# One matmul of 490 columns per pair, three banks in turn, for a graph network's relation adjacency

## The chip, the cores and the metric

The kernel runs on one core of a Trainium2 chip. The metric is the device time of one launch in microseconds (us). The kernel before was timed in three runs: 7019.02, 7025.52 and 7033.47 us, median 7025.52.

Engine names are those of the profile: PE is TensorE (PEld its weight loads), DVE VectorE, ACT ScalarE, POOL GpSimd, SP SyncE. The granted TensorE clock is given as a share of full speed; it has two levels, 0.5 (1.2 GHz) and 1.0 (2.4 GHz), and a mean over a stretch lies between them.

## The reference, cut to what matters

6250 nodes with 128 features, 206,250 edges. Each edge has one of five types (relations), each node one of three types.

```
x = layernorm(x + SAGE(SAGE(x)))            # two SAGE layers, mean over incoming edges
h = concat(x, node_emb[node_type])          # 256 features
h = relu(rgcn(h, W1, root1))                # 256 -> 256
h = relu(rgcn(h, W2, root2))                # 256 -> 128
h = rgcn(h, W3, root3)                      # 128 -> 128
out = layernorm(x + relu(h))

def rgcn(x, W, root):                       # per destination node n, per relation r
    agg[n, r] = mean of x[src] over edges into n with type r
    return sum_r agg[n, r] @ W[r] + x @ root + bias
```

## The kernel before, in words

The kernel sorts and codes the edges, runs the two SAGE layers (up to about 1480 us in the profile), and then the three relational layers, which the code calls conv 0, 1 and 2. Conv 0 ends near 4150 us.

**Groups.** In conv 0, edges are taken 512 at a time (a *group*, 403 in all). POOL fetches the source rows of a group with four indirect DMAs (L1395) into `messages`, a ring of six groups: POOL may fetch group i only when PE has finished group i-6 (`group_psum`). DVE makes a one-hot matrix of the group's destinations (L1669). PE multiplies the two, 12 matmuls of 120 columns (L1408) and four narrow ones for the node types (L1412), which raise `group_psum`. DVE adds the result to running sums (`add`, L1690 and L1691); PE needs `sums_added` of two groups back.

**Windows.** The sums of 256 nodes (a *window*, about 16 groups) are finished in 12 steps, n = 0 to 11, one per *half tick*; there are two half ticks to a group. At step 0 DVE scales the sums (`scale`, L1730, then two memsets and `node_hot`), and SP copies the scaled type sums to other partitions with six small DMAs (L1305). At step 1 PE computes the 256 wide features in two halves (L1495, L1496; between the halves it waits for SP's copies, `typed_in`, before L1493). ACT evicts them into `h_wide` (L1601). At step 3 PE computes the next layer's root part (L1502, bank 5) and then the first tile of the next layer's table (`table`, L1473, banks 6 and 7). At step 4 ACT evicts both (L1605, L1582), at step 5 DVE takes the remainder (L1747), at step 6 PE computes the second tile.

**The relations' adjacency.** Beside this, 336 of the 403 groups each carry two *couples*, and a couple is two *pairs* of nodes. For each pair DVE makes two one-hot matrices (L1678, L1679) and PE multiplies them (`build`, L1428); the result, 128 x 490 counts, is cast to 8 bits and stored for convs 1 and 2. The 490 columns are five relations of 98. Before the change they are cut in two parts, 250 and 240 columns, for the two halves of the node tiles: a couple is four matmuls, two of 250 columns (both pairs) into bank 2 and two of 240 into bank 3. ACT evicts bank 2 (L1558) and DVE bank 3 (L1560) into `stage`; every eight couples ACT stores a stage to memory (L1572). Each bank is used by every couple, so a couple's first matmul waits for ACT's eviction of the couple before, and its third for DVE's.

**Order.** All engines run the same loop over half ticks, written out at build time, and each engine keeps its order. PE in an even half tick: group, build, window step; in an odd one: build, window step. DVE: eviction of the couple of the half tick before, then (even) one-hots and `add` or (odd) the pairs' one-hots, then the window step. ACT: eviction of this half tick's couple, then the window step. Step 0 falls on an odd half tick, so step 1 follows a group and a build on PE, and on DVE the eviction that this build waited for stands behind step 0.

Of the kernel before, what the change touches and what calls it, by code (L numbers as in the profile page):

```python
# [176 lines left out]
def resnorm_gnn(nc, a, out):  # L177
# [27 lines left out]
    with ctx:  # L205
# [1011 lines left out]
        REL_BANKS, PART_BANKS = DENSE_BANKS, TABLE_BANKS  # L1217
# [180 lines left out]
        def conv_tensor(pe):  # L1398
# [17 lines left out]
            def build(j):  # L1416

                b, m = divmod(2 * j, BATCH)
                if m == 0:
                    pe.wait_ge(rel_hot_made, b + 1)  # L1420
                for n in range(SLICES):
                    if j:
                        pe.wait_ge(rel_evicted[n], j)
                    of_part = slice(2 * SLICE_FIRST[n], 2 * (SLICE_FIRST[n] + SLICE_TILES[n]))
                    width = 2 * SLICE_TILES[n] * RELATIONS
                    for q in range(2):
                        hot = rel_hot[:, b % 2, m + q, :].rearrange("p (r c) -> p r c", r=RELATIONS)[:, :, of_part]
                        mm = pe.matmul(bank[REL_BANKS[n]][:, q * width:(q + 1) * width], lo_dense_hot[:, b % 2, m + q, :], hot, start=True, stop=True)  # L1428
                    mm.then_inc(rel_psum, 1)

            def dense(v, step):
# [8 lines left out]
                if at == 0:  # L1440
                    if K >= 2:
                        pe.wait_ge(dense_kept, K - 1)
                    else:
                        pe.wait_ge(rel_evicted[K], COUPLES)
# [21 lines left out]
            def table(w, t):  # L1466
                n = w * WINDOW_TILES + t
                pe.wait_ge(wide_made, w + 1)
                pe.wait_ge(rest_made, ROW_SPLITS + n)
                nodes = slice(t * P, (t + 1) * P)  # L1470
                for b, cols in enumerate((slice(0, FIRST_CUT), slice(FIRST_CUT, RELATIONS * FEAT))):
                    for half in range(2):
                        mm = pe.matmul(bank[TABLE_BANKS[b]][:, 0:cols.stop - cols.start], h_wide[:, half, nodes], w2[:, half, cols], start=(half == 0), stop=(half == 1))  # L1473
                mm.then_inc(table_psum, 1)

            def finish(v, i, n):
# [4 lines left out]
                if v == 0:  # L1481
# [16 lines left out]
                    if n == 3:  # L1498
                        pe.wait_ge(wide_made, w + 1)
                        pe.wait_ge(root_kept, w)  # L1500
                        for half in range(2):
                            mm = pe.matmul(bank[ROOT_BANK][:, 0:cols], w2_root[:, half, :], h_wide[:, half, 0:cols], start=(half == 0), stop=(half == 1))  # L1502
                        mm.then_inc(root_psum, 1)
                        table(w, 0)
# [43 lines left out]
        def evict(engine, n, j):  # L1548

            u, m = divmod(j, STAGE_COUPLES)  # L1550
            engine.wait_ge(rel_psum, j * SLICES + n + 1)
            if m == 0 and u >= 2:
                engine.wait_ge(stage_out[u % 2], 16 * SLICES * (u // 2))
            rows = slice(RELATIONS * SLICE_FIRST[n], RELATIONS * (SLICE_FIRST[n] + SLICE_TILES[n]))
            from_bank = bank[REL_BANKS[n]][:, 0:4 * SLICE_TILES[n] * RELATIONS].rearrange("p (q c d) -> p c q d", q=2, d=2)
            to = stage[:, u % 2, rows, 4 * m:4 * m + 4].rearrange("p c (q d) -> p c q d", q=2)
# [5 lines left out]
        def conv_scalar(act):  # L1562
            def store_stage(u):
# [3 lines left out]
                for n in range(SLICES):  # L1567
                    width = SLICE_TILES[n] * STAGE_NODES
                    first = SLICE_FIRST[n] * CHUNK + s * width
                    rows = slice(RELATIONS * SLICE_FIRST[n], RELATIONS * (SLICE_FIRST[n] + SLICE_TILES[n]))  # L1570
                    of_part = stage[:, u % 2, rows, :].rearrange("p (r h) d -> p r (h d)", r=RELATIONS).bitcast(bf16)
                    act.dma_start(relations_d[c, :, :, first // 2:(first + width) // 2], of_part).then_inc(stage_out[u % 2], 16)  # L1572

            def row_pieces(w, t, step):
                n = w * WINDOW_TILES + t
                rows = table_rows[:, n % 2, :].rearrange("p (r k f) -> p r k f", r=RELATIONS, f=P)
                if step == 0:
# [3 lines left out]
                    for b, at_r, count in ((0, 0, 3), (1, 3, 2)):  # L1581
                        op = act.copy(rows[:, at_r:at_r + count, 0, :], bank[TABLE_BANKS[b]][:, 0:count * P].rearrange("p (r f) -> p r f", f=P))  # L1582
# [5 lines left out]
            def finish(v, i, n):  # L1588
# [4 lines left out]
                if v == 0:  # L1593
# [9 lines left out]
                    if n == 4:  # L1603
                        act.wait_ge(root_psum, w + 1)
                        act.activation(root_part[:, nodes], bank[ROOT_BANK][:, 0:cols], ACT.Identity, bias=bias[:, 4:5]).then_inc(root_kept, 1)  # L1605
# [55 lines left out]
        def conv_vector(vec):  # L1661
# [78 lines left out]
            def row_pieces(w, t, at_step):  # L1740
                n = w * WINDOW_TILES + t
                rows = table_rows[:, n % 2, :].rearrange("p (r k f) -> p r k f", r=RELATIONS, f=P)
                if at_step == 0:
                    vec.wait_ge(high_made, ROW_SPLITS + n + 1)
                    vec.wait_ge(low_made, ROW_SPLITS + n)
                    for b, at_r, count in ((0, 0, 3), (1, 3, 2)):
                        op = vec.tensor_tensor(rest_w[:, at_r * P:(at_r + count) * P].rearrange("p (r f) -> p r f", f=P),  # L1747
                                               bank[TABLE_BANKS[b]][:, 0:count * P].rearrange("p (r f) -> p r f", f=P), rows[:, at_r:at_r + count, 0, :], ALU.subtract)
# [436 lines left out]
```

## Time and profile before

| | |
|---|---|
| median of three runs | 7025.52 us (7019.02 to 7033.47) |
| span of the profiled execution | 7027.7 us |
| PE busy | 4925.6 us (70%) |
| POOL busy | 3636.8 us (52%) |
| DVE busy | 2875.6 us (41%) |
| ACT busy | 1023.1 us (15%) |
| mean granted TensorE clock | 0.842 |

The span is 2.2 us above the median and within the range of the runs; the page shows nothing of that execution outside its span. Shares of the whole span mix stages: the change acts on conv 0 alone, and there a view cut to 1480 to 3720 us (groups with builds) and one to 3720 to 4150 us (the last groups, without builds, and the end of the last windows) tell more.

### The profile page before, as it was taken

Reading aid. Unit: us, or ns where it says so; the run is one execution under the profiler, and the core shown is the slowest. Engines: PE = TensorE matmul, PEld = TensorE weight load, DVE = VectorE, ACT = ScalarE, POOL = GpSimd, SP = SyncE. Lnnn points to the kernel's source line nnn. Section 1 sums busy time; section 2 is a strip of 40 time slices with the busy share of each in tenths; the row PEclk is TensorE's granted clock in tenths of the full one; section 3 lists DMA queues with packets and bytes.
Section 4 is the critical chain, followed back from the end, with each engine's and each line's share of the span. In section 5 each row is a group of like instructions: output and inputs, shape, how many; then the busy total and the mean of one; then the engine's idle time right before and its main releaser. Section 6 shows DMA issues by size and latency. Waiting matters only on the chain.

```text
span 7027.7 us, 95103 instructions
## 1 busy us (share of the span) xinstructions
PE 4925.6 (70%) x35932; PEld 3076.0 (44%) x35932; DVE 2875.6 (41%) x8139; ACT 1023.1 (15%) x2385; POOL 3636.8 (52%) x3575
## 2 busy tenths in 40 slices
PE   2776789955655655656554448888888788888887
PEld 1544556633333333333333334444444445544544
DVE  5766661136666666666662211111112212111212
ACT  2544440002222222212220000000000000000000
POOL 4000000036666666666666646666666566666664
PEclk6888889977777777777776669999999899999999
DMA  2222216543434434434343334554545444444443
GB/s 77 96 111 100 90 64 227 219 135 113 121 106 120 120 105 122 119 112 117 114 116 97 97 116 134 168 167 148 169 137 167 154 138 146 138 139 147 142 135 104
DMA packets 428468, 904.12 MB, mean 129 GB/s; under 512 B 71170, under 2 KB 335116, under 8 KB 406124
## 3 DMA queue, kind: packets, MB, share of 16 engines
q0 software_dynamic: 169216, 348.44, 18.4%
q1 hardware_dynamic: 129028, 454.04, 17.7%
q10 hardware_dynamic: 129768, 95.53, 4.3%
q8 instruction: 289, 4.73, 0.3%
q14 instruction: 167, 1.37, 0.1%
HBM read 692.22 MB, written 205.05 MB: 128 GB/s over the span
## 4 chain that ended last, share of the span: by engine, by line
PE 43%; another core or an unknown queue 15%; issue 9%; DVE 8%; ACT 2%; DVEq 1%; DMA 0%; SPq 0%; ACTq 0%; POOL 0%; POOLq 0%
PE bank L1450 23%; PE bank L1408 7%; PE bank L1428 5%; PE bank L1495 2%; PE bank L1473 2%; PE bank L1412 2%; ACT stage L1558 1%; DVE stage L1560 1%; DVE scaled L1730 1%; DVE rel_hot L1679 1%; DVE type_scaled L1730 1%; DVE lo_dense_hot L1678 1%; DVE sums L1691 1%; DVE sums L1737 1%
## 5 line engine op out<-in xcount | busy, mean ns | idle before, releaser
L1395 POOL DMA_INDIRECT messages<-table,src_rows x2552 | 2653.3, 1040 | 1384.9 <-issue 692.0
L1450 PE MATMUL bank<-slices,pieces 128*128 128x384 fp8e4 x10290 | 1978.4, 337 | 375.5 <-issue 361.2
L1450 PEld LDWEIGHTS bank<-slices,pieces 128*128 128x128 bf16 x10290 | 988.8, 100 | 1211.6 <-issue 704.5
L1428 PE MATMUL bank<-rel_hot,lo_dense_hot 128*128 128x240 bf16 (+1 forms) x2688 | 589.2, 331 | 914.5 <-ACT stage L1558 463.2
L1395 POOL DMA_INDIRECT messages<-table,rel_rows x940 | 899.5, 957 | 560.8 <-issue 250.7
L1691 DVE TENSOR_TENSOR sums<-sums,bank 128x120 f32 x873 | 236.4, 271 | 2292.1 <-remote 1826.1
L1408 PE MATMUL bank<-group_hot,messages 128*128 128x120 bf16 x10476 | 832.5, 239 | 238.8 <-issue 112.8
L1408 PEld LDWEIGHTS bank<-group_hot,messages 128*128 128x128 bf16 x10476 | 747.4, 111 | 357.1 <-issue 204.8
L1428 PEld LDWEIGHTS bank<-rel_hot,lo_dense_hot 128*128 128x128 bf16 x2688 | 193.0, 106 | 1243.6 <-ACT stage L1558 532.2
L1377 POOL IOTA iota_rel_i<- 128x490 int32 x1 | 1.4, 1394 | 1355.2 <-DMA table<-typed_rows 1355.2
L1558 ACT CAST stage<-bank 128x500 fp8e4<-128x500 f32 x672 | 387.2, 576 | 1772.5 <-PE bank L1428 1094.9
L1560 DVE CAST stage<-bank 128x480 fp8e4<-128x480 f32 x672 | 435.0, 647 | 242.7 <-PE bank L1428 219.4
L877 PE MATMUL bank<-adjacency,x_pieces 128*128 128x384 bf16 (+1 forms) x2499 | 485.2, 336 | 0.0
L1679 DVE TENSOR_SCALAR rel_hot<-iota_rel,rel_dense 128x490 bf16<-128x490 f16 x1344 | 468.5, 349 | 0.0
L975 ACT CAST adjacency<-bank 128x400 bf16<-128x400 f32 x784 | 392.0, 504 | 440.4 <-PE bank L853 434.4
L1690 DVE TENSOR_TENSOR type_sums<-type_sums,bank 3x120 f32 x403 | 107.1, 266 | 812.0 <-remote 591.9
L853 PE MATMUL bank<-q_hot,lo_hot 128*128 128x100 bf16 x3136 | 230.9, 222 | 267.5 <-DVE rd_hot L1057 258.8
L877 PE MATMUL bank<-adjacency,h_pieces 128*128 128x384 bf16 (+1 forms) x2499 | 398.9, 320 | 0.0
L1678 DVE TENSOR_SCALAR lo_dense_hot<-iota,lo_dense 128x128 bf16<-128x128 f16 x1344 | 354.9, 264 | 0.0
L1669 DVE TENSOR_TENSOR group_hot<-iota,group_code 128x480 bf16<-128x480 f16 x873 | 349.5, 401 | 1.6
L853 PEld LDWEIGHTS bank<-q_hot,lo_hot 128*128 128x128 bf16 x3136 | 193.1, 105 | 344.3 <-DVE rd_hot L1057 258.7
L877 PEld LDWEIGHTS bank<-adjacency,h_pieces 128*128 128x128 bf16 x2499 | 238.5, 98 | 151.8 <-issue 3.8
(251 smaller groups left out, 3593.3 us busy)
## 6 DMA issues: line engine op xcount, KB each, us to landing
slices<-relations_d SPq DMA_DIRECT2D x70, 1200.0 KB
slices<-relations_d SPq DMA_DIRECT2D x70, 1152.0 KB
adjacency_d<-adjacency SPq DMA_DIRECT2D x15, 4704.0 KB, 14.5
adjacency<-adjacency_d SPq DMA_DIRECT2D x15, 4704.0 KB, 15.0
relations_d<-stage ACTq DMA_DIRECT2D x84, 500.0 KB
messages<-table,src_rows POOLq DMA_INDIRECT x2552
relations_d<-stage ACTq DMA_DIRECT2D x84, 480.0 KB
inverse<-inverse_d SPq DMA_DIRECT2D x52, 640.0 KB
```

The source lines that it names most:

```text
L853: mm = pe.matmul(to[:, m * PAIR_COLS:(m + 1) * PAIR_COLS], lo_hot[:, i % 2, pair, :], q_hot[:, i % 2, pair, :], start=True, stop=True)
L877: mm = pe.matmul(bank[SUM_BANKS[k % 2]][:, 0:cols], pieces[:, h, piece, :], adjacency[HALF[c]][:, h, 0:cols], start=(m == 0), stop=(m == N ...
L975: act.copy(to, pairs).then_inc(evicted, 1)
L1395: pool.indirect_dma_start(messages[:, i % MESSAGES, t, 0:ROWS[v]], None, GATHERED[v], bass.IndirectOffsetOnAxis(ap=rows[:, e:e + 1], axis= ...
L1408: mm = pe.matmul(to[:, 0:GROUP_COLS], messages[:, i % MESSAGES, t, piece * P:(piece + 1) * P], group_hot[:, i % MESSAGES, t, :], start=(t ...
L1428: mm = pe.matmul(bank[REL_BANKS[n]][:, q * width:(q + 1) * width], lo_dense_hot[:, b % 2, m + q, :], hot, start=True, stop=True)
L1450: mm = pe.matmul(bank[DENSE_BANKS[K % 2]][:, 0:CHUNK], pieces[M % PIECE_RING][:, tile % PIECE_TILES, piece * P:(piece + 1) * P], slice_of_ ...
L1558: engine.copy(to, from_bank, saturate=False).then_inc(rel_evicted[n], 1)
L1560: engine.tensor_copy(to, from_bank, saturate=False).then_inc(rel_evicted[n], 1)
L1669: vec.tensor_tensor(group_hot[:, i % MESSAGES, :, :].rearrange("p k (c t) -> p k c t", t=2), iota16[:, 0:GROUP_COLS].rearrange("p (c t) -> ...
L1678: vec.tensor_scalar(lo_dense_hot[:, b % 2, m, :], iota16[:, :], lo_dense[:, b * BATCH + m:b * BATCH + m + 1], None, ALU.is_equal)
L1679: op = vec.tensor_scalar(rel_hot[:, b % 2, m, :], iota_rel[:, :], rel_dense[:, b * BATCH + m:b * BATCH + m + 1], None, ALU.is_equal)
```

## The change

Each pair becomes one matmul of 490 columns into a bank of its own. Three banks (2, 3, 5) are taken in turn; ACT evicts the even pair of each couple and DVE the odd one. Since the banks rotate by three and the evictions by two, an even pair's matmul waits for DVE's eviction of the odd pair two couples back, an odd pair's for ACT's eviction of the couple before. `stage` holds the 245 rows in one block; an eviction writes two bytes per row where it wrote four, and the store to memory reads the two parts out of the block.

Bank 5 had been the root part's. The root part now sits in columns 0 to 255 of bank 6, and the table's second part in columns 256 to 511 of it. So the table waits for ACT's eviction of the root part (`root_kept`), the root part waits until DVE has read the tables of the window before, and the table's first tile moves from step 3 to step 4.

```diff
-        REL_BANKS, PART_BANKS = DENSE_BANKS, TABLE_BANKS
+        PART_BANKS = TABLE_BANKS
+        REL_BANKS = (2, 3, 5)
+        ROOT_1 = bank[6][:, 0:WINDOW]
+        TABLES_1 = (bank[7][:, 0:3 * P], bank[6][:, WINDOW:WINDOW + 2 * P])
...
-                for n in range(SLICES):
-                    if j:
-                        pe.wait_ge(rel_evicted[n], j)
-                    of_part = slice(2 * SLICE_FIRST[n], 2 * (SLICE_FIRST[n] + SLICE_TILES[n]))
-                    width = 2 * SLICE_TILES[n] * RELATIONS
-                    for q in range(2):
-                        hot = rel_hot[:, b % 2, m + q, :].rearrange("p (r c) -> p r c", r=RELATIONS)[:, :, of_part]
-                        mm = pe.matmul(bank[REL_BANKS[n]][:, q * width:(q + 1) * width], lo_dense_hot[:, b % 2, m + q, :], hot, start=True, stop=True)
-                    mm.then_inc(rel_psum, 1)
+                for q in range(2):
+                    pair = 2 * j + q
+                    before = pair - len(REL_BANKS)
+                    if before >= 0:
+                        pe.wait_ge(rel_evicted[before % 2], before // 2 + 1)
+                    pe.matmul(bank[REL_BANKS[pair % len(REL_BANKS)]][:, 0:REL_COLS], lo_dense_hot[:, b % 2, m + q, :], rel_hot[:, b % 2, m + q, :],
+                              start=True, stop=True).then_inc(rel_psum, 1)
...
                 pe.wait_ge(rest_made, ROW_SPLITS + n)
+                pe.wait_ge(root_kept, w + 1)
...
                         pe.wait_ge(wide_made, w + 1)
-                        pe.wait_ge(root_kept, w)
+                        pe.wait_ge(rest_made, ROW_SPLITS + w * WINDOW_TILES)
                         for half in range(2):
-                            mm = pe.matmul(bank[ROOT_BANK][:, 0:cols], w2_root[:, half, :], h_wide[:, half, 0:cols], start=(half == 0), stop=(half == 1))
+                            mm = pe.matmul(ROOT_1[:, 0:cols], w2_root[:, half, :], h_wide[:, half, 0:cols], start=(half == 0), stop=(half == 1))
                         mm.then_inc(root_psum, 1)
+                    if n == 4:
                         table(w, 0)
...
-            engine.wait_ge(rel_psum, j * SLICES + n + 1)
+            pair = 2 * j + n
+            engine.wait_ge(rel_psum, pair + 1)
...
-            rows = slice(RELATIONS * SLICE_FIRST[n], RELATIONS * (SLICE_FIRST[n] + SLICE_TILES[n]))
-            from_bank = bank[REL_BANKS[n]][:, 0:4 * SLICE_TILES[n] * RELATIONS].rearrange("p (q c d) -> p c q d", q=2, d=2)
-            to = stage[:, u % 2, rows, 4 * m:4 * m + 4].rearrange("p c (q d) -> p c q d", q=2)
+            from_bank = bank[REL_BANKS[pair % len(REL_BANKS)]][:, 0:REL_COLS].rearrange("p (c d) -> p c d", d=2)
+            to = stage[:, u % 2, :, 4 * m + 2 * n:4 * m + 2 * n + 2]
...
```

What PE has in its order around the first window's step 1, before the change (`scaled_144` is the window's scaled sums, `bank4` the wide features, `rel_evicted0` ACT's evictions and `rel_evicted1` DVE's):

```order
L1412 MATMUL bank1<-group_hot_147,messages_146 3x120 x4
L1428 MATMUL bank2<-rel_hot_154,lo_dense_hot_153 128x250 [waits rel_evicted0,rel_hot_made]
L1428 MATMUL bank2<-rel_hot_154,lo_dense_hot_153 128x250
L1428 MATMUL bank3<-rel_hot_154,lo_dense_hot_153 128x240 [waits rel_evicted1]
L1428 MATMUL bank3<-rel_hot_154,lo_dense_hot_153 128x240
L1495 MATMUL bank4<-scaled_144,w1_126 128x256 [waits wide_made,emb_in,scaled_made]
```

And after it:

```order
L1415 MATMUL bank1<-group_hot_147,messages_146 3x120 x4
L1429 MATMUL bank2<-rel_hot_154,lo_dense_hot_153 128x490 [waits rel_evicted1,rel_hot_made]
L1429 MATMUL bank3<-rel_hot_154,lo_dense_hot_153 128x490 [waits rel_evicted0]
L1498 MATMUL bank4<-scaled_144,w1_126 128x256 [waits wide_made,emb_in,scaled_made]
L1498 MATMUL bank4<-scaled_144,w1_126 128x256 x4
```

Four matmuls of the build became two, and the wait for `rel_evicted1` in front of the wide features is now for an eviction one couple older.

PE around steps 3 and 4 of the same window before the change (`w2_root_129` marks the root part, `w2_128` the table):

```order
L1428 MATMUL bank3<-rel_hot_154,lo_dense_hot_153 128x240
L1502 MATMUL bank5<-h_wide_142,w2_root_129 128x256 [waits root_kept,wide_made]
L1502 MATMUL bank5<-h_wide_142,w2_root_129 128x256
L1473 MATMUL bank6<-w2_128,h_wide_142 128x384 [waits rest_made,wide_made]
L1473 MATMUL bank6<-w2_128,h_wide_142 128x384
L1473 MATMUL bank7<-w2_128,h_wide_142 128x256 x2
L1428 MATMUL bank2<-rel_hot_154,lo_dense_hot_153 128x250 [waits rel_evicted0]
```

And after it:

```order
L1505 MATMUL bank6<-h_wide_142,w2_root_129 128x256 [waits rest_made,wide_made]
L1505 MATMUL bank6<-h_wide_142,w2_root_129 128x256
L1429 MATMUL bank2<-rel_hot_154,lo_dense_hot_153 128x490 [waits rel_evicted1]
L1429 MATMUL bank3<-rel_hot_154,lo_dense_hot_153 128x490 [waits rel_evicted0]
L1476 MATMUL bank7<-w2_128,h_wide_142 128x384 [waits root_kept,rest_made,wide_made]
L1476 MATMUL bank7<-w2_128,h_wide_142 128x384
L1476 MATMUL bank6<-w2_128,h_wide_142 128x256 x2
L1411 MATMUL bank1<-group_hot_147,messages_146 128x120 [waits gathered5,group_hot_made,sums_added]
```

The table's first tile moved behind the next couple's build, and it now waits for `root_kept`, an eviction that ACT makes in the same half tick.

## Rows read from the trace of the kernel before

**Rows 1.** Stretches: us, then busy us (instructions) per engine, granted clock, DMA share, GB/s.
```profile
1480.00:3720.00 2240.00, 1300.16 (x9074) 819.94 (x9075) 1454.38 (x4642) 459.36 (x855) 1505.97 (x1379) 0.74 0.40 116
3720.00:4150.00 430.00, 179.47 (x1258) 132.62 (x1258) 105.08 (x261) 20.36 (x44) 239.93 (x241) 0.64 0.31 87
```

**Rows 2.** Waits of POOL, 1480 to 3720 us: us in total, times, longest.
```profile
POOL messages L1395 <- issue: 376.6, 1233, 0.5
POOL messages L1395 <- PE bank L1412: 203.3, 64, 9.2
POOL messages L1395 <- remote: 147.6, 81, 4.4
```

**Rows 3.** Waits of PE in the same stretch.
```profile
PE bank L1428 <- ACT stage L1558: 463.2, 187, 19.1
PE bank L1428 <- DVE stage L1560: 233.0, 163, 8.7
```

**Rows 4.** POOL's groups (busy us, mean ns | idle), 1480:3720, then 3720:4020.
```profile
L1395 POOL DMA_INDIRECT messages<-table,src_rows x1378 | 1505.1, 1092 | 727.5 <-issue 376.6 <-PE bank L1412 203.3 <-remote 147.6
...
L1395 POOL DMA_INDIRECT messages<-table,src_rows x197 | 198.2, 1006 | 103.1 <-issue 55.8 <-remote 25.2 <-PE bank L1412 22.1
```

**Rows 5.** Stretches between two stops of POOL that end with "remote".
```profile
2224.90:2242.80 17.90, 9.31 (x72) 5.56 (x72) 10.90 (x40) 3.49 (x7) 12.61 (x12) 0.69 0.36 108
...
3741.40:3770.30 28.90, 8.44 (x80) 6.49 (x80) 3.87 (x15) 0.00 (x0) 19.14 (x20) 0.56 0.27 69
4809.50:4821.40 11.90, 9.58 (x71) 5.39 (x69) 2.33 (x7) 0.00 (x0) 7.57 (x8) 1.00 0.55 186
```

**Rows 6.** Timeline of a window with builds: start, us, instruction, idle before and releaser.
```profile
2285.81 2.36 DVE L1730 TENSOR_TENSOR scaled<-sums,inverse 128x1280 f32<-128x1280 f32 x1
...
2288.05 2.40 DVE L1730 TENSOR_TENSOR type_scaled<-type_sums,inverse 3x1280 f32<-3x1280 f32 x1
...
2294.24 0.58 PE L1428 MATMUL bank<-rel_hot,lo_dense_hot 128*128 128x240 bf16 x2 [8.65 <-DVE stage L1560]
...
2294.62 4.48 PE L1495 MATMUL bank<-scaled,w 128*128 128x256 f32 x10
...
2299.72 0.29 PEld L1493 LDWEIGHTS bank<-type_scaled,emb 18*128 18x128 f32 x2 [0.49 <-DMA type_scaled<-node_hot]
...
2300.34 2.42 PE L1495 MATMUL bank<-scaled,w 128*128 128x256 f32 x10
...
2305.56 0.94 POOL L1395 DMA_INDIRECT messages<-table,src_rows  x1 [6.49 <-PE bank L1412]
...
2308.68 0.59 PE L1428 MATMUL bank<-rel_hot,lo_dense_hot 128*128 128x250 bf16 x4
...
2311.59 0.94 POOL L1395 DMA_INDIRECT messages<-table,src_rows  x1 [1.21 <-PE bank L1412]
```

**Rows 7.** Timeline of a window without builds.
```profile
3783.84 4.32 PE L1495 MATMUL bank<-scaled,w 128*128 128x256 f32 x10 [8.45 <-DVE type_scaled L1730]
...
3792.63 1.22 PE L1493 MATMUL bank<-type_scaled,emb 18*128 18x256 f32 x2 [4.04 <-DMA type_scaled<-node_hot]
...
3793.78 4.47 PE L1495 MATMUL bank<-scaled,w 128*128 128x256 f32 x10
...
3801.21 0.94 POOL L1395 DMA_INDIRECT messages<-table,src_rows  x1 [2.84 <-PE bank L1412]
```

**Rows 8.** Stretches from L1493 to the end of the wide features.
```profile
2299.70:2303.75 4.05, 4.05 (x17) 2.78 (x16) 0.00 (x0) 0.00 (x0) 0.00 (x0) 1.00 0.12 29
3792.60:3799.20 6.60, 6.57 (x16) 4.45 (x16) 0.00 (x0) 0.00 (x0) 4.54 (x5) 0.59 0.33 83
```

**Rows 9.** Line L1605, the root part's eviction, 1480 to 3720 us: ns min/median/max.
```profile
L1605 ACT ACTIVATE root_part<-bank,bias x20: 479/479/479, 1660.8 to 3709.4; 128x256 f32<-128x256 f32 x20
```

**Rows 10.** The page's groups: busy us, mean ns, then idle us before.
```profile
L1558 ACT CAST stage<-bank 128x500 fp8e4<-128x500 f32 x672 | 387.2, 576 | 1772.5 <-PE bank L1428 1094.9
L1560 DVE CAST stage<-bank 128x480 fp8e4<-128x480 f32 x672 | 435.0, 647 | 242.7 <-PE bank L1428 219.4
```

## What the change should do to the time: the prediction

> **What bounds the kernel now.** I cut the trace by stage first. The change acts on conv 0, and nearly all of it on the 2240 us in which groups carry builds [rows 1]. PE is busy for 1300 us of them, DVE for 1454, ACT for 459: none is full. POOL is busy for 1506 us, has another 377 us in short pauses between two issues, and waits for 351 us: 203 us for PE's L1412, the last matmul of a group, and 148 us for "remote" [rows 2]. The first two make 1883 us, the third 351 us; together that is the stage. The gathers are in order and POOL waits for nothing else, so POOL paces conv 0. The time moves by what the change does to those 351 us and to POOL's own work, and by nothing else.
>
> Then I read PE's waits. PE waits 463 us for ACT's evictions and 233 us for DVE's [rows 3]. This is what the change takes away, and it looks like a tenth of the run. The reader is to see that these 696 us are not POOL's 351 us. POOL waits for a finished group when its ring of six is full, and most of PE's waits fall where PE is ahead of POOL anyway.
>
> The third view is the pace where nothing else disturbs it. POOL stops for "remote" about every third group. From stop to stop PE does 72 matmuls in 17.9 us with builds (12 fetches, three groups), 80 in 28.9 us without builds (20 fetches, five groups), 71 in 11.9 us in conv 1 (eight fetches, two groups) [rows 5]. That is 5.97, 5.78 and 5.95 us per group. Two things follow. The stops seem to come with a count of PE's instructions; what they are, these rows don't tell. And the pace per group hardly depends on what PE has to do: taking all builds away from PE, DVE and ACT gains 0.19 us per group.
>
> The fourth view is one window's timeline. POOL's long stop, 6.49 us, falls here: DVE scales from 2285.81 on, PE stands 8.65 us at a build for the DVE eviction behind that, then does the wide features, and only the next group releases POOL [rows 6]. There are 20 such windows in the stage [rows 9]. Twenty times 6.49 is 130 of the 203 us.
>
> **The change part by part.**
>
> *Builds.* Of four matmuls per couple two go, but no columns: 980 before and after. A couple takes 0.59 us at full clock [rows 6]. A matmul of 490 columns is not in the trace; I bound a couple between 0.4 us (980 columns at 2.4 GHz) and 0.6. It saves at most 0.2 us x 672 = 134 us of PE work, all of it beside POOL's fetches. In the sum: 0. If the cover were gone, 0.2 us per build behind a POOL stop, a few us.
>
> *Evictions.* ACT goes from 500 to 490 elements (576 ns), DVE from 480 to 490 (647 ns) [rows 10]. By elements that is -0.01 and +0.01 us. Two-byte writes at a step of 32 bytes are not in the trace; DVE's scaling reads with a step at 2360 ns for 1280 elements [rows 6], 1.84 ns each against 1.35 here, so at worst a DVE eviction costs 0.9 us, 0.25 more. DVE is busy for 1454 of 2240 us; two evictions per group, 0.5 us of 5.97, disappear in its idle time. In the sum: 0, at worst about 0.25 us x 20 in front of the windows.
>
> *Waits of PE on evictions.* Gone nearly everywhere. What is late next between windows is POOL itself. The gain is bounded by the no-build pace: 0.19 us x about 240 groups that lie between the windows (336 less 20 x 5) = 46 us; nothing excludes a zero. A group now has 20 matmuls in place of 24, a third of the way to the 16 without builds, and no eviction waits, so I take half of 46: -23 us.
>
> *The wide features.* Here the wait of 8.65 us goes and another takes its place. PE can start the first half as soon as DVE has scaled, at 2288.05 + 2.40 = 2290.45 in place of 2294.62. But the second half needs SP's copies, and those hang on DVE alone: L1493's weights already waited 0.49 us for the DMA in this window [rows 6]. So the second half starts at most 0.5 us earlier, and PE stands for some 4 us in front of it. The windows without builds show that very situation: first half right behind the scaling, then 4.04 us of idling for the DMA, then the same ten matmuls of L1495 in 4.47 us where they took 2.42 [rows 6, 7]. The granted clock is 0.59 in that stretch, 1.00 in the window with builds, and the way from L1493 to the end of the wide features takes 6.60 us against 4.05 [rows 8]. That is 2.55 us more less up to 0.5: 2.1 us per window, in front of the group that releases POOL. 20 x 2.1 = +42 us. Bounds: 0 if the clock holds, 20 x 2.55 = +51.
>
> The Trainium skill speaks against this part too: "TensorE: Matmul & The Clock Gate", section "HAM oscillation — how this bites in real kernels", says that a wait for a DMA between two bursts of matmuls sends the array back to half clock, burst after burst. By that rule every one of the 20 windows pays, 20 x 2.1; the trace agrees with it in the stretch at 0.59 [rows 8].
>
> *Root part and table.* The table's first tile now stands behind a build and behind ACT's eviction of the root part. PE before: root, table, build (0.59 us), next group [rows 6]. After: root, build, wait, table, group. The wait: ACT first evicts the even pair of that same build (0.3 us until its matmul is done, 0.58 us of work), then the root part (0.48 us) [rows 9, 10], and a few tenths for semaphores: 1.45 us from the root's end, of which the build covers 0.5 to 0.6. So the table starts 0.85 us later than PE could. Behind it waits the second group of the window, and POOL stood 1.21 us for that group [rows 6], where a plain pause is 0.3. So it is on the path: 20 x 0.85 = +17 us. Bounds 0 and 20 x 1.45 = +29. DVE's L1747 and the second tile move by the same, not once more. In the last windows, without builds, only ACT's 0.48 us count, and at the very end alone they are on the path: +1. The new wait of the root part on the tables of the window before is long met.
>
> *Stores, bank reuse later.* The store has the same bytes and the same number of pieces. Convs 1 and 2 use banks 2, 3, 5, 6 as before, after all evictions. 0.
>
> Sum: -23 + 42 + 17 + 1 = +37 us. The profiled span is 7027.7, 2 us above the median; applied to the median 7025.5 it gives 7062. Its own range, with the bounds: from 7025 - 46 + 0 + 0 = 6980 to 7025 + 0 + 51 + 29 = 7105; more narrowly 7040 to 7085.
>
> **The rivals.**
>
> *Faster: PE gets to the window with POOL less far ahead.* Without builds POOL's stop at the window is 2.84 us, not 6.49, although the clock is down there too [rows 6, 7]. The reason is that PE had come closer to POOL by then, so the ring had more room. If the shorter build does the same by half, each window gains (6.49 - 2.84) / 2 = 1.8 us plus the 2.1 us that I charged, and pays 0.85: against my sum -3.9 x 20 = -78, so 7062 - 78 = 6984. For it: 20 matmuls per group in place of 24 fit the count of 72 with 3.6 groups, so stops may come every fourth group. Against it: between stops DVE has 10.90 / 3 = 3.6 us of work per group that stays [rows 5], and a fetch by POOL takes 1092 ns with builds against 1006 without [rows 4]. Over four fetches that is 0.34 us per group, more than the 0.19 by which the pace differs. On this the Trainium skill has a rule, "SBUF — State Buffer", section "Who interferes with whom": DVE in its two-port modes locks GpSimd out for a whole instruction, while PE and ACT wait for nobody. By it the gain without builds is DVE's, whose work the change leaves, and this rival would be worth nothing; the means of rows 4 agree with it but do not prove it.
>
> *No change.* The clock drops, but POOL's stop is as long as before because the lag of PE shrinks by as much, and the root wait hides in POOL's "remote" stop right behind it: -23 + 42 - 20 = about 0, 7025.
>
> *More slower than I say.* If PE's idling lowers the clock in every group too (mean 0.74 with builds, 0.64 without [rows 1]) and the couple behind the window too runs at the lower level, 1.2 GHz, its 0.59 us [rows 6] become twice that, 0.6 us per window more. With no gain between windows: 42 + 17 + 12 = +71, about 7100.
>
> **How the numbers follow.** Sum as worked out or more (slower): 0.47, of which 0.10 for the last rival. No change: 0.20. Faster by the lag: 0.33, for the stops are not understood and I have only a count for them. I forecast 7060 us. The likeliest case alone lies in 7040 to 7085; the range for 8 in 10 reaches to the faster rival and past it, 6975, and up to 7100. Within 0.2% (14 us) no change can be told by this measurement: faster 0.33, same 0.20, slower 0.47.
>
> **What would show it.** Right: PE's waits for L1558 and L1560 fall by most of their 696 us, and POOL's waits in the stage stay near 351 us or grow. In a window, a DMA wait of about 4 us in front of L1496 (the old L1493) and ten matmuls in over 4 us at a clock near 0.6. The table waits about 0.9 us for ACT. Wrong: the clock stays 1.0 from L1496 to the end of the wide features; POOL's long stop at the windows falls under 4 us; or stops come with 60 matmuls or fewer, or 80 and more, so that the pace between windows leaves 5.8 to 6.0 us per group.

## The result, and the profile after

The changed kernel takes 7081.4 us (median of four runs, 7077.5 to 7087.9), the kernel before 7026.9 beside it: ratio 1.0079, 95% interval 1.0066 to 1.0092, 55 us slower. The forecast was 7060 and slower. The direction was right, and three terms came out near what they were given at. Yet the largest single cost of the change had been put at nothing, and a gain that it hid was underrated by some 56 us.

The stage first. These are the stretches of [rows 1] in the changed kernel (us; then busy us and instructions of PE, PEld, DVE, ACT, POOL; granted clock, DMA share, GB/s):

```profile
1480.00:3720.00 2240.00, 1325.46 (x7568) 737.38 (x7569) 1677.27 (x4561) 837.53 (x836) 1509.52 (x1354) 0.71 0.40 114
3720.00:4150.00 430.00, 192.80 (x1335) 137.74 (x1334) 127.29 (x325) 30.58 (x49) 263.69 (x260) 0.64 0.32 89
```

1506 PE instructions fewer (1344 are the builds', over all 672 couples; the rest is the slower pace in a stretch of the same length), and yet DVE is busy for 223 us more and ACT for 378. The page's groups say why (busy us, mean ns, then idle us before); they answer to [rows 10]:

```profile
L1429 PE MATMUL bank<-rel_hot,lo_dense_hot 128*128 128x490 bf16 x1344 | 569.9, 491 | 726.5 <-ACT stage L1562 372.5
L1562 ACT CAST stage<-bank 128x490 fp8e4<-128x490 f32 x672 | 793.1, 1233 | 1383.6 <-PE bank L1429 764.8
L1564 DVE CAST stage<-bank 128x490 fp8e4<-128x490 f32 x672 | 793.8, 1181 | 196.2 <-PE bank L1429 182.0
```

An eviction takes 1.23 us on ACT where it took 0.58, and 1.18 on DVE where it took 0.65, for the same number of elements.

POOL's waits, 1480 to 3760 us (the stage with builds is 42 us longer now); they answer to [rows 2]:

```profile
POOL messages L1398 <- issue: 386.3, 1261, 1.8
POOL messages L1398 <- PE bank L1415: 237.4, 50, 13.0
POOL messages L1398 <- remote: 117.2, 60, 4.3
```

PE's waits in the same stretch, which answer to [rows 3]:

```profile
PE bank L1429 <- ACT stage L1562: 370.1, 196, 11.6
...
PE bank L1498 <- DVE type_scaled L1734: 82.3, 20, 4.8
...
PE bank L1496 <- DMA type_scaled<-node_hot: 66.6, 20, 4.0
PE bank L1429 <- DVE stage L1564: 53.4, 80, 1.3
PE bank L1476 <- ACT root_part L1609: 26.4, 19, 1.4
```

Of the 696 us of waits on evictions 273 went, and 175 came in three new places: the scaling, SP's copies, the root part's eviction.

And one window's timeline, the counterpart of [rows 6] (start, us, instruction, idle before and releaser):

```profile
2305.03 4.63 PE L1498 MATMUL bank<-scaled,w 128*128 128x256 f32 x10 [4.38 <-DVE type_scaled L1734]
...
2313.45 0.69 PE L1496 MATMUL bank<-type_scaled,emb 18*128 18x256 f32 x2 [2.94 <-DMA type_scaled<-node_hot]
...
2314.08 4.11 PE L1498 MATMUL bank<-scaled,w 128*128 128x256 f32 x10
...
2319.18 0.59 PE L1429 MATMUL bank<-rel_hot,lo_dense_hot 128*128 128x490 bf16 x2
...
2320.97 1.08 POOL L1398 DMA_INDIRECT messages<-table,src_rows  x1 [7.12 <-PE bank L1415]
...
2324.36 2.39 PE L1476 MATMUL bank<-w,h_wide 128*128 128x384 f32 x8 [1.39 <-ACT root_part L1609]
...
2327.96 0.95 POOL L1398 DMA_INDIRECT messages<-table,src_rows  x1 [2.03 <-PE bank L1415]
```

It is the picture that was forecast: first half right behind the scaling, PE waiting for SP's copies, ten matmuls in 4.11 us (2.42 before), then the table behind ACT's eviction of the root part. In the second half's ten matmuls the granted clock is 0.59, mostly the lower level, and the way from L1496 to the end of the wide features takes 5.8 us (4.05 in [rows 8]). This window is among the shortest: over the 20 windows the way is 6.74 us on average (5.8 to 7.4), where it was 4.11 before, and PE waits 3.3 us for the copies. The two stretches of this window:

```profile
2313.40:2319.20 5.80, 5.75 (x17) 3.95 (x18) 0.00 (x0) 0.00 (x0) 0.46 (x1) 0.71 0.11 29
...
2314.05:2318.20 4.15, 4.15 (x12) 3.33 (x12) 0.00 (x0) 0.00 (x0) 0.00 (x0) 0.59 0.09 24
```

For a budget I follow POOL from its first fetch to its 1344th (336 groups), fetch by fetch, and sort its pauses. *First stop*: the longest at each window; *second*: the one four fetches later; *other*: all further pauses above 1.1 us.

| us, 1st to 1344th fetch | before | changed | |
|---|---|---|---|
| fetches (mean ns) | 1466.4 (1092) | 1498.5 (1116) | +32.1 |
| first stops, 19 windows | 129.1 | 177.3 | +48.2 |
| second stops | 23.1 | 36.4 | +13.3 |
| other stops (count) | 175.5 (90) | 122.1 (63) | -53.4 |
| short pauses | 379.2 | 381.5 | +2.3 |
| together | 2173.3 | 2215.8 | +42.5 |

Behind the 1344th fetch conv 0 takes 11.4 us more, 6 of them the 20th window's two stops; convs 1 and 2 together 1 us less.

### The profile page after: what moved, and what is told of

The parts are those of the page before. It is cut to its first block, busy times and chain, and to the rows that moved or that the text cites. A ratio compares the mean times of both kernels' runs of the same rounds, so it can differ in the third digit from the quotient of the medians.

```text
span 7082.4 us, 92417 instructions
## 1 busy us (share of the span) xinstructions
PE 5000.6 (71%) x34588; PEld 3029.4 (43%) x34588; DVE 3132.6 (44%) x8139; ACT 1418.6 (20%) x2385; POOL 3674.9 (52%) x3575
## 4 chain that ended last, share of the span: by engine, by line
PE 35%; DVE 18%; another core or an unknown queue 11%; issue 10%; ACT 1%; SPq 1%; DVEq 1%; DMA 1%; POOL 0%; ACTq 0%; POOLq 0%
PE bank L1452 22%; DVE stage L1564 6%; PE bank L1411 5%; DVE rel_hot L1683 3%; DVE lo_dense_hot L1682 2%; PE bank L1498 2%; PE bank L1476 1%; DVE scaled L1734 1%; DVE group_hot L1673 1%; SPq L1308 1%; DVE sums L1695 1%; PE bank L1429 1%; DVE type_scaled L1734 1%; DVEq L1688 1%
## 5 line engine op out<-in xcount | busy, mean ns | idle before, releaser
L1398 POOL DMA_INDIRECT messages<-table,src_rows x2552 | 2687.4, 1053 | 1402.8 <-issue 703.1
L1429 PE MATMUL bank<-rel_hot,lo_dense_hot 128*128 128x490 bf16 x1344 | 569.9, 491 | 726.5 <-ACT stage L1562 372.5
L1562 ACT CAST stage<-bank 128x490 fp8e4<-128x490 f32 x672 | 793.1, 1233 | 1383.6 <-PE bank L1429 764.8
L1411 PE MATMUL bank<-group_hot,messages 128*128 128x120 bf16 x10476 | 858.4, 242 | 260.7 <-issue 136.2
L1564 DVE CAST stage<-bank 128x490 fp8e4<-128x490 f32 x672 | 793.8, 1181 | 196.2 <-PE bank L1429 182.0
L1429 PEld LDWEIGHTS bank<-rel_hot,lo_dense_hot 128*128 128x128 bf16 x1344 | 106.7, 102 | 1100.2 <-ACT stage L1562 464.6
L1682 DVE TENSOR_SCALAR lo_dense_hot<-iota,lo_dense 128x128 bf16<-128x128 f16 x1344 | 332.3, 247 | 0.0
L1498 PE MATMUL bank<-scaled,w 128*128 128x256 f32 (+1 forms) x500 | 220.6, 626 | 124.8 <-DVE type_scaled L1734 124.8
```

Source lines behind the costliest of these rows:

```text
L1398: pool.indirect_dma_start(messages[:, i % MESSAGES, t, 0:ROWS[v]], None, GATHERED[v], bass.IndirectOffsetOnAxis(ap=rows[:, e:e + 1], axis= ...
L1411: mm = pe.matmul(to[:, 0:GROUP_COLS], messages[:, i % MESSAGES, t, piece * P:(piece + 1) * P], group_hot[:, i % MESSAGES, t, :], start=(t ...
L1429: pe.matmul(bank[REL_BANKS[pair % len(REL_BANKS)]][:, 0:REL_COLS], lo_dense_hot[:, b % 2, m + q, :], rel_hot[:, b % 2, m + q, :], start=Tr ...
L1562: engine.copy(to, from_bank, saturate=False).then_inc(rel_evicted[n], 1)
L1564: engine.tensor_copy(to, from_bank, saturate=False).then_inc(rel_evicted[n], 1)
L1682: vec.tensor_scalar(lo_dense_hot[:, b % 2, m, :], iota16[:, :], lo_dense[:, b * BATCH + m:b * BATCH + m + 1], None, ALU.is_equal)
```

## The experiments

The kernel before took 6971 and 6974 us in the two sets that hold e0 to e7 and 7029 in the one with e8 and e9, so the ratio to its own set is what is compared. The changed kernel, timed again in the second set (e0), stands at 1.0067, and e1, e2, e3 and e5, from the first set, are compared with it all the same. The sets differ behind conv 0 above all: the changed kernel takes 2915 us there in e0 and 2953 in its first profile, but 2214 and 2216 for the 1344 fetches, so the stops can be set side by side. The stops are means over 20 windows; "other" as above.

| run | ratio (95%) | first | second | other (count) | fetch ns |
|---|---|---|---|---|---|
| before, again (e8) | 1.0000 (0.9990 to 1.0010) | 7.49 | 1.21 | 190.1 (94) | 1081 |
| changed, again (e0) | 1.0067 (1.0052 to 1.0083) | 9.82 | 1.83 | 112.6 (54) | 1113 |
| e1 root in bank 4 | 1.0021 (1.0009 to 1.0032) | 8.45 | 0.86 | 118.0 (59) | 1114 |
| e2 packed evictions | 0.9961 (0.9946 to 0.9975) | 4.79 | 1.05 | 109.7 (42) | 1129 |
| e3 wide before wait | 0.9921 (0.9904 to 0.9938) | 4.54 | 1.99 | 111.0 (52) | 1114 |
| e4 warm gap | 1.0013 (1.0003 to 1.0024) | 7.72 | 1.89 | 104.4 (47) | 1111 |
| e5 four matmuls | 1.0088 (1.0059 to 1.0116) | 8.69 | 1.90 | 116.2 (52) | 1127 |
| e6 couples by engine | 0.9985 (0.9969 to 1.0001) | 6.46 | 0.36 | 106.3 (45) | 1126 |
| e7 both | 0.9859 (0.9841 to 0.9877) | 3.37 | 1.02 | 108.0 (47) | 1111 |
| e9 before, wide first | 0.9971 (0.9959 to 0.9983) | 7.00 | 1.18 | 197.6 (98) | 1084 |

**e0 and e8, the two kernels again.**

> The changed kernel itself, beside the other runs on their chip, so that stages can be compared. Its ratio to the kernel before should be the 1.0079 measured first, within its interval of 0.0013; first stop of a window 9.45 us, second 1.92, all other stops of the stage 122 us.

> The kernel before, profiled on the chip of the experiments, so that its stages can be set beside those of the changed kernel there: ratio 1.000 within 0.002; first stop of a window near 6.8 us, second near 1.2, the other stops of the stage 165 to 180 us, and the stage without builds, 411.5 us on the first chip, tells whether the 11 us by which the changed kernel was longer there are the change's.

Both ratios are as expected. The stops are not all: the other stops of the kernel before are 190.1 us, above the 165 to 180 expected (175.5 in its first profile), those of the changed kernel 112.6 (122.1). This shows how far one profile can be trusted; the mean first stop of the kernel before is 6.78 in one and 7.49 in the other. The 11 us in the stage without builds are not settled: it is 411.8 us in the changed kernel's second profile, against 411.5 and 407.9 in the kernel before, so most of them need not be the change's.

**e2, packed evictions.**

```diff
-            to = stage[:, u % 2, :, 4 * m + 2 * n:4 * m + 2 * n + 2]
+            whole = stage[:, u % 2, :, :].rearrange("p c d -> p (c d)")
+            to = whole[:, (2 * m + n) * REL_COLS:(2 * m + n + 1) * REL_COLS].rearrange("p (c d) -> p c d", d=2)
```

> The changed kernel with each eviction writing its 490 bytes as one run in the stage, not two bytes every 32; the order of the stored counts is thereby another one, the amount the same. Theory A (evictions that took 1.18 and 1.23 us in place of 0.65 and 0.58 do so because of the two-byte pieces, and cost through DVE: POOL's fetch 1116 ns in place of 1092, 32 us over 1343 fetches, and DVE's scaling 0.74 us later against POOL, 15 us over 20 windows): an eviction falls to 0.55 to 0.65 us, and the time to about 7034. Rival 1 (the doubled evictions are hidden beside POOL): evictions fall, the time stays at 7075 to 7085. Rival 2 (490 columns from a bank in one go are slow to read): evictions stay at 1.2 us.

```profile
L1563 ACT CAST stage<-bank 128x490 fp8e4<-128x490 f32 x672 | 378.2, 572 | 1669.2 <-PE bank L1429 844.9
L1565 DVE CAST stage<-bank 128x490 fp8e4<-128x490 f32 x672 | 437.1, 650 | 233.4 <-PE bank L1429 162.4
```

The same reads and the same bytes, written in one run: 0.57 and 0.65 us. So the two-byte pieces double an eviction. They cost 1.0067 - 0.9961, 1.1% or 74 us; without them the change would have been 0.4% faster than before. (This kernel leaves out the reordering that convs 1 and 2 would need, so its output is not the network's; its stages have the same work, and what follows conv 0 takes 2919 us, 2915 in e0. A usable form without two-byte pieces is e6.) Theory A holds in its main point and fails in one: fetches did not become faster (1129 ns), so the cost does not run through them. It is in the stops at the windows: the first is 5.0 us shorter than in e0, the second 0.8. The rows point to PE: behind a window it has a backlog and is held up by evictions, as here in the changed kernel:

```profile
2328.04 2.24 ACT L1562 CAST stage<-bank 128x490 fp8e4<-128x490 f32 x2 [0.49 <-PE bank L1429]
...
2329.29 0.38 PE L1429 MATMUL bank<-rel_hot,lo_dense_hot 128*128 128x490 bf16 x1 [0.87 <-ACT stage L1562]
...
2334.99 0.38 PE L1429 MATMUL bank<-rel_hot,lo_dense_hot 128*128 128x490 bf16 x1 [1.51 <-ACT stage L1562]
```

From the window's first group to the sixth behind it PE takes 31.2 us in the changed kernel and 29.0 with packed evictions (means over the windows). At the next window's scaling POOL is 4.2 groups ahead of PE in the first and 3.1 in the second; the ring holds six. The first stop begins 12.3 us behind the scaling's start in the changed kernel, and 18.1 here. That slow evictions cost 74 us is shown; the way over PE's six groups is argued, for in e6 PE takes only some 27 us for them and POOL is 3.6 groups ahead all the same.

**e3, wide before wait.**

```diff
-                        to = [bank[WIDE_BANK][:, half * WINDOW:half * WINDOW + cols] for half in range(2)]
+                        pe.wait_ge(rest_made, ROW_SPLITS + w * WINDOW_TILES)
+                        to = [bank[b][:, 0:cols] for b in (WIDE_BANK, 7)]
...
-                                pe.wait_ge(typed_in, 16 * (RELATIONS + 1) * (w + 1))
-                                pe.matmul(to[0], emb_all[:, f_cols[0]], typed_all[:, 0:cols], start=False, stop=True)
...
+                        pe.wait_ge(typed_in, 16 * (RELATIONS + 1) * (w + 1))
+                        pe.matmul(to[0], emb_all[:, f_cols[0]], typed_all[:, 0:cols], start=False, stop=True)
                         pe.matmul(to[1], emb_all[:, f_cols[1]], typed_all[:, 0:cols], start=False, stop=True).then_inc(window_psum, 1)
...
```

> The changed kernel with the ten matmuls and the x part of the wide features' second half put ahead of the wait for SP's copies, into bank 7, which is free then; behind the wait only the four small matmuls of the types are left. Theory A (the stop of PE for that DMA with half of the work behind it, at a low clock, is what a window costs): the wide features end 10 to 12 us after DVE's scaling in place of 15.2, 3.3 to 5.3 us x 20 = 65 to 105 us: 6975 to 7015, below the kernel before. Rival (the long stop of POOL is set by how late DVE scales and adds, not by the end of the wide features): 7075 to 7085.

1.5% below the changed kernel, 102 us: theory A at the top of its range. A window's timeline:

```profile
2269.86 4.04 PE L1495 MATMUL bank<-scaled,w 128*128 128x256 f32 x10 [4.35 <-DVE type_scaled L1733]
...
2274.17 2.32 PE L1495 MATMUL bank<-scaled,w 128*128 128x256 f32 x10
...
2278.80 0.69 PE L1498 MATMUL bank<-type_scaled,emb 18*128 18x256 f32 x2 [1.88 <-issue]
2279.34 0.59 PE L1499 MATMUL bank<-type_scaled,emb 18*128 18x256 f32 x2
...
2282.88 0.95 POOL L1398 DMA_INDIRECT messages<-table,src_rows  x1 [2.00 <-PE bank L1415]
```

Twenty matmuls fit into the wait, the second ten in 2.32 us right behind the first, and little is left behind the copies. On average the wide features end 14.6 us behind the scaling's start, 20.3 in the changed kernel beside it.

**e4, warm gap.**

```diff
                             if half:
+                                if w:
+                                    pe.wait_ge(rest_made, ROW_SPLITS + w * WINDOW_TILES)
+                                for r in range(RELATIONS):
+                                    pe.matmul(bank[7][:, 0:cols], w1[:, r, f_cols[1]], scaled[:, r, 0:cols], start=True, stop=True)
                                 pe.wait_ge(typed_in, 16 * (RELATIONS + 1) * (w + 1))
```

> The changed kernel with ten further matmuls (the products of the second half, into bank 7, thrown away) between the wide features' first half and the wait for SP's copies, so that PE idles less there. Theory A (the second half is slow because PE stood idle and its clock had fallen): the second half takes 2.4 us in place of 4.1 and the way from L1496 to the end 4.1 us in place of 6.74; if the further matmuls end before the copies land this gives 2.6 us per window, 53 us, if they overrun by a us, 30 us: 7028 to 7050. Rival (the clock is low there whatever stood ahead): the way stays at 6.7, the overrun costs, 7080 to 7105.

0.54% below the changed kernel, 38 us, by nothing but work that is thrown away. A window's timeline, and the stretch from L1499 (the old L1496) to the end of the wide features:

```profile
2289.00 2.32 PE L1497 MATMUL bank<-scaled,w 128*128 128x256 f32 x10
2292.69 0.69 PE L1499 MATMUL bank<-type_scaled,emb 18*128 18x256 f32 x2 [1.36 <-DMA type_scaled<-node_hot]
2293.31 2.42 PE L1501 MATMUL bank<-scaled,w 128*128 128x256 f32 x10
```

```profile
2292.65:2296.75 4.10, 4.06 (x17) 2.81 (x18) 0.00 (x0) 0.00 (x0) 0.00 (x0) 1.00 0.02 4
```

The clock is 1.00 where it was 0.71 in the changed kernel's same stretch, 4.1 us in place of 5.8. Only half of the windows look like this one. In ten of the 20 the way is 4.1 us, behind waits for the copies of 1.2 us on average; in the other ten it is 5.8, behind waits of 2.3 us, as here:

```profile
1969.94 0.69 PE L1499 MATMUL bank<-type_scaled,emb 18*128 18x256 f32 x2 [2.49 <-DMA type_scaled<-node_hot]
1970.56 4.11 PE L1501 MATMUL bank<-scaled,w 128*128 128x256 f32 x10
```

```profile
1969.90:1975.75 5.85, 5.81 (x17) 4.05 (x18) 0.00 (x0) 0.00 (x0) 0.66 (x1) 0.71 0.13 34
```

So theory A's 4.1 us are reached in half of the windows, and the gain lies in its range without the overrun that the range allowed for. On average the way is 4.9 us, 6.8 in e0. PE's idling and the clock are thus shown as the cause of the slow second half, at about 2 us per window: 1.9 x 20 is the 38 us.

**e1, root in bank 4.**

```diff
-        ROOT_1 = bank[6][:, 0:WINDOW]
-        TABLES_1 = (bank[7][:, 0:3 * P], bank[6][:, WINDOW:WINDOW + 2 * P])
+        ROOT_1 = bank[WIDE_BANK][:, 0:WINDOW]
+        TABLES_1 = (bank[6][:, 0:3 * P], bank[7][:, 0:2 * P])
...
-                pe.wait_ge(root_kept, w + 1)
...
+                        pe.wait_ge(root_kept, w)
...
-                    if n == 4:
                         table(w, 0)
```

> The changed kernel with the root part in the wide features' bank 4 (free once they are evicted), so that the table has banks 6 and 7 to itself and stands at step 3 again without a wait for ACT. Theory A (the table behind ACT's eviction of the root part is on POOL's path): the stop of POOL for the second group of a window falls from 1.92 us to about 1.2, 20 x 0.7 = 14 us, and some 4 us more in the windows without builds: 7062 to 7068. Rival (that second stop is the group's own lag behind the long stop): it stays near 1.9 and the time at 7081.

The second stop goes as expected (1.83 to 0.86 us), the time by more, 0.46% or 32 us. The first stop is 1.4 us shorter than in e0 too; that is within twice what two profiles of one kernel differ by, so where the rest comes from stays open.

**e5, four matmuls.**

```diff
-                    pe.matmul(bank[REL_BANKS[pair % len(REL_BANKS)]][:, 0:REL_COLS], lo_dense_hot[:, b % 2, m + q, :], rel_hot[:, b % 2, m + q, :],
-                              start=True, stop=True).then_inc(rel_psum, 1)
+                    for cols in (slice(0, 250), slice(250, REL_COLS)):
+                        mm = pe.matmul(bank[REL_BANKS[pair % len(REL_BANKS)]][:, cols], lo_dense_hot[:, b % 2, m + q, :], rel_hot[:, b % 2, m + q, cols], start=True, stop=True)
+                    mm.then_inc(rel_psum, 1)
```

> The changed kernel with each pair's matmul cut into 250 and 240 columns, both in the pair's own bank: 24 matmuls per group again, with three banks and the same evictions. Theory A (POOL's stops between windows come with a count of PE's matmuls, about 72): the stops come every third group again and the 62 us that they gave back return, less what POOL's slower fetches hide: 7105 to 7145. Rival (the gain between windows is that PE no longer waits for evictions): stops as in the changed kernel, 7075 to 7090.

24 matmuls per group again, and the other stops stay at 116 us in 52: the count of matmuls is not what sets them. Its ratio can't be told from the changed kernel's. So the stops between windows became fewer with what else the change does, not with fewer matmuls. The root part (e1) and the evictions (e2) leave them as few too; of the change that leaves the banks in turn, which no run takes away alone.

**e6 and e7, couples by engine, and both.** In e6 and e7 bank 6 belongs to the builds, so the root part and the table's second part share bank 4:

```diff
-                    pe.matmul(bank[REL_BANKS[pair % len(REL_BANKS)]][:, 0:REL_COLS], ...
+                    pe.matmul(rel_banks[j % 2][:, 512 * q:512 * q + REL_COLS], ...
...
+            if j % 2 != n:
+                return
...
-            to = stage[:, u % 2, :, 4 * m + 2 * n:4 * m + 2 * n + 2]
+            from_bank = rel_banks[n][:, :].rearrange("p (q c) -> p q c", q=2)[:, :, 0:REL_COLS].rearrange("p q (c d) -> p c q d", d=2)
+            to = stage[:, u % 2, :, 4 * m:4 * m + 4].rearrange("p c (q d) -> p c q d", q=2)
```

> The changed kernel with two pairs of banks, (2, 3) and (5, 6): a couple fills a pair of banks, ACT evicts every even couple and DVE every odd one, 980 bytes in runs of four. The root part and the table's second part move to bank 4, and ACT evicts the root part at step 3. Theory A (runs of two bytes are what made evictions slow): an eviction of 980 takes about twice that of 490 in one run, 1.14 us on ACT and 1.30 on DVE, as much per couple as before the change; the stage's stops are then those of the run with packed evictions (4.8, 1.05, 110 us) and the ratio to the kernel before 0.993 to 0.997. Rival (the gain of that run came from the single run of 490 bytes, and any stride of 32 costs): 2.4 us per eviction, ratio 1.00 to 1.01.

> The couples by engine, as in the run beside it, and the wide features' second half ahead of the wait for SP's copies. Theory A (the two costs of a window, late evictions on DVE and the wide features behind the DMA, lie one behind the other): the first stop falls from 4.8 us by most of what the second half's move gave alone, to 1 to 2 us, 20 x 3 = 60 us more: ratio 0.985 to 0.990. Rival (both took away the same part of the stop, and what is left is set by DVE's scaling): first stop 4 to 5 us, ratio 0.991 to 0.996.

The evictions in e6, now of a whole couple:

```profile
L1568 ACT CAST stage<-bank 128x980 fp8e4<-128x980 f32 x336 | 328.0, 976 | 1375.7 <-remote 694.5
L1570 DVE CAST stage<-bank 128x980 fp8e4<-128x980 f32 x336 | 389.9, 1160 | 234.5 <-PE bank L1432 179.1
```

Twice the elements in four-byte runs take less time than 490 in two-byte runs. The run of bytes decides, not the step of 32. The ratio, 0.9985 (its interval reaches 1.0001, so it is not clear of the kernel before), is above the range that was expected: POOL is 3.6 groups ahead at the scaling, not 3.1, and the first stop is 6.5 us, not 4.8. Why this arrangement catches up less than the packed one is open. With the wide features' order of e3 the ratio is 0.9859, in the range, and the first stop 3.37 us, above the 1 to 2 expected. This version beats both kernels, the one before by 1.4%, the changed one by 2.1%. POOL's waits in its stage with builds, 1480 to 3560 us:

```profile
POOL messages L1403 <- issue: 380.2, 1245, 0.6
POOL messages L1403 <- remote: 107.7, 50, 4.2
POOL messages L1403 <- PE bank L1420: 91.7, 50, 6.9
```

**e9, the order of e3 in the kernel before.** The diff is that of e3.

> The kernel before, with the wide features' second half ahead of the wait for SP's copies, as in the run that made the changed kernel 110 us faster. Theory A (that gain exists only where PE reaches the first half right behind DVE's scaling; here PE starts it 4.2 us later, behind DVE's eviction, and the copies land while it works): the wide features end where they did, 0 to 0.5 us earlier per window, 0 to 10 us: ratio 0.998 to 1.000; the windows without builds, five, gain 3 us each at most. Rival (the order alone is worth it, whatever the evictions do): 60 to 110 us, ratio 0.985 to 0.991.

0.3%, 20 us: a little more than theory A allowed, and a fifth of what the same edit gives in the changed kernel. The order is worth most where the eviction wait in front of the first half is gone.

## Why the prediction was right, and where it was not

*What bounds the kernel: right.* The 42.5 us of the stage are POOL's stops and fetches; PE's waits on evictions were not the measure. They fell from 696 us to 424 (370.1 for L1562, 53.4 for L1564, to 3760 us), less than "most of their 696 us", and the kernel became slower, while POOL's waits stayed at 355 us (351 before).

*Builds, 0: right.* A couple takes 0.59 us as before. The idea that POOL's stops come with a count of PE's matmuls is wrong (e5).

*Evictions, 0: wrong; this is the step that failed.* "By elements that is -0.01 and +0.01 us ... so at worst a DVE eviction costs 0.9 us": it is 1.18, and ACT's 1.23. The bound came from the scaling, four-byte elements read with a step; a row with byte pieces there was not, and ACT was given no bound at all. The second half of the step failed as well: two evictions "disappear in its idle time". DVE and ACT do have idle time on average, but in the backlog behind a window PE stands for them. The price is 74 us (e2), where the step had 0 and at worst 0.25 us x 20. The Trainium skill, "Advanced Engine Details and Errata", section "Memory Cachelines", says that an access to another line of 16 bytes than the one before is penalised, and that at least two hits on a line are needed to absorb the latency. Here two bytes per line cost double and four did not: the direction agrees, and if each byte is a hit, two were not enough.

*Between windows, -23: near, made of other parts.* Other stops -53, fetches +32, short pauses +2: -19. That POOL's fetches would slow down was not foreseen. The mean is 1081 and 1092 in the kernel before and 1111 to 1129 in every form of the changed one, with short evictions too (e2), so it is not the eviction's length; what it is, is open. That -19 stands where -23 was forecast is thus in part luck.

*Wide features, +42: right.* From the scaling's start to the end of the wide features it is 18.08 us before and 20.00 after, 1.9 x 20 = 38. The way from L1496 took 2.63 us more (6.74 less 4.11) where 2.55 was read from the windows without builds. The mechanism is shown by e4 and e3. The first stops grew by somewhat more (48 in 19 windows), which two profiles of one kernel can differ by.

*Root and table, +17: near, with help from the step that failed.* The second stop grew by 0.70 us, 14 in all; undoing it gave 32 (e1), so it may cost more than the stop that shows it. But the table waits 1.39 us for ACT, not 0.9, for ACT's slow eviction of the even pair stands in front of the root part's. With packed evictions (e2) the wait is 0.92 us, as forecast, and the second stop 1.05 us, no longer than before (1.22): the wait alone did not show in POOL's stop there.

*Rival "PE gets to the window with POOL less far ahead": its mechanism exists.* With short evictions POOL is a group less ahead and the first stop is 4.79 us, below before, though the wide features end as late as in the changed kernel. The rival said 0.6% faster, e2 shows 0.4%. The slow evictions took that gain away; had they been seen, the sum of the text, too poor in gains, would have been 37 + 74 = 111 us, twice the 55 measured. The total was near because two errors cancelled, and that is luck.

## What to carry to other kernels

Look at the runs of bytes that a rewritten access pattern leaves in its destination before counting its elements: halving them from four to two doubled an eviction here. An engine that is idle on average can still cost when another has a backlog behind it, so price an engine's added time where the backlog is. And when a wait in front of a burst goes, move the work that needs nothing from the next wait ahead of it: that order was worth 1.5% in the changed kernel, more than the whole change cost, and 0.3% in the kernel before.

## What the hardware showed that was not expected

Casting 490 float32 from a bank to 8-bit takes 0.57 us on ACT and 0.65 on DVE written in one run, and 1.23 and 1.18 written two bytes in every 32; 980 elements four bytes in every 32 take 0.98 and 1.16. Ten matmuls per window whose results nobody used made the kernel 0.5% faster (e4), though they kept the clock at 1.00 in half of the windows only.
